# A selective-scan layer rearranged: channel halves outside, states inside, decays in PSUM, rows of B by DMA

## The reference

```python
x_dbl = jnp.einsum('bld,ed->ble', x, x_proj_w)        # x: layer-normed stream
delta_r = x_dbl[..., :DT_RANK]
B = x_dbl[..., DT_RANK:DT_RANK + D_STATE]
C = x_dbl[..., DT_RANK + D_STATE:]
delta = jax.nn.softplus(jnp.einsum('blr,dr->bld', delta_r, dt_proj_w) + dt_proj_b)
A = -jnp.exp(A_log)
dA = jnp.exp(delta[..., None] * A[None, None])
dBu = (delta * u)[..., None] * B[:, :, None, :]
def step(h, inp):
    dA_t, dBu_t, C_t = inp
    h = dA_t * h + dBu_t
    y_t = jnp.einsum('bdn,bn->bd', h, C_t)
    return (h, y_t)
return y + u * D[None, None, :]
```

## Time and profile before

| | us |
|---|---|
| median of 3 runs | 1988.52 (1988.13 to 1989.62) |
| the profiled execution, its own time | 1987.44 |
| its span in the trace | 1985.3 |
| the scan layer, first operation to last | 567.3 to 768.9 |
| its loop, first scan to last product | 610.4 to 759.35 |

### The profile page before, as it was taken

The page is one execution under the profiler, slowest core; times in us unless marked ns, Lnnn a source line. Parts: engine busy times, 40 slices in busy tenths (PEclk is TensorE's granted clock), DMA queues, the critical chain, the costliest instruction groups (busy, mean ns, idle before and its releaser), DMA issues. The chain is left out here.

```text
span 1985.3 us, 27571 instructions
## 1 busy us (share of the span) xinstructions
PE 1594.6 (80%) x9254; PEld 1163.6 (59%) x9254; DVE 1139.6 (57%) x2139; ACT 924.4 (47%) x1940; POOL 758.8 (38%) x699
## 2 busy tenths in 40 slices
PE   6999789778964656274899999999999999999373
PEld 5444578667841224263677677767777667776362
DVE  4665454755468996445655655556554665554533
ACT  2456334323524332243556555555665556665342
POOL 3011251215067674315633444344433443430603
PEclk9899789879977887596999999999999999999587
DMA  3222233223310003342000000000000000000443
GB/s 81 47 47 84 80 119 110 59 72 123 109 39 0 0 0 99 121 127 78 11 15 12 11 9 9 17 12 6 11 12 12 9 9 12 9 6 1 154 139 106
DMA packets 79204, 98.10 MB, mean 49 GB/s; under 512 B 12112, under 2 KB 63824, under 8 KB 79072
## 3 DMA queue, kind: packets, MB, share of 16 engines
q1 hardware_dynamic: 72928, 79.59, 13.8%
q0 software_dynamic: 6144, 16.79, 2.7%
HBM read 62.25 MB, written 27.66 MB: 45 GB/s over the span
## 5 line engine op out<-in xcount | busy, mean ns | idle before, releaser
L1307 DVE TENSOR_SCALAR_CACHE_REDUCE gqa_scaled<-acc,gqa_neg_scale 128x128 bf16<-128x128 f32 (+7 forms) x256 | 208.9, 816 | 312.4 <-PE acc L1459 311.0
L1479 PE MATMUL aux<-gqa_probsT,gqa_v 128*128 128x512 f32 (+3 forms) x768 | 272.1, 491 | 11.2 <-DVE gqa_turned_k L1263 7.0
L1200 ACT ACTIVATE gqa_probsT<-aux 128x512 f32<-128x512 f32 (+3 forms) x384 | 174.6, 491 | 188.0 <-PE aux L1470 188.0
L1190 ACT ACTIVATE gqa_probs<-acc,gqa_bias,gqa_q_scale 128x128 f32<-128x128 f32 (+7 forms) x256 | 213.7, 835 | 46.3 <-DVE gqa_scaled L1307 39.9
L1084 POOL TENSOR_TENSOR gqa_q_high<-gqa_straight,gqa_turned_q 128x512 fp32r<-128x512 f32 x64 | 87.7, 1370 | 327.7 <-DVE gqa_turned_q L1263 327.7
L1479 PEld LDWEIGHTS aux<-gqa_probsT,gqa_v 128*128 128x128 f32 x768 | 138.1, 190 | 103.1 <-issue 62.2
L1470 PE MATMUL aux<-ident,gqa_probs 128*128 128x128 f32 x1152 | 168.9, 274 | 0.3 <-ACT gqa_probsT L1200 0.3
L1458 PE MATMUL acc<-gqa_k_high,gqa_q_high 128*128 128x512 f32 (+3 forms) x384 | 156.4, 407 | 7.3 <-DVE gqa_k_low L1291 5.7
L1458 PE MATMUL acc<-gqa_k_high,gqa_q_low 128*128 128x512 f32 (+3 forms) x384 | 133.3, 347 | 0.0
L1458 PE MATMUL acc<-gqa_k_low,gqa_q_high 128*128 128x512 f32 (+3 forms) x384 | 132.9, 346 | 0.0
L1470 PEld LDWEIGHTS aux<-ident,gqa_probs 128*128 128x128 f32 x1152 | 124.7, 141 | 0.6 <-issue 0.4
(11 more groups left out here) (411 smaller groups left out, 4329.5 us busy)
## 6 DMA issues: line engine op xcount, KB each, us to landing
f_w<-in_f_up SPq DMA_DIRECT2D x64, 256.0 KB, 2.7
f_xs<-tokens_by_slot SPq DMA_DIRECT2D x108, 128.0 KB, 2.2
outputs_by_slot<-f_y_tile SPq DMA_DIRECT2D x108, 128.0 KB, 1.7
f_w<-in_f_down SPq DMA_DIRECT2D x64, 128.0 KB, 3.0
mat_qk<-mat_high SPq DMA_DIRECT2D x64, 64.0 KB, 2.3
gqa_w_q<-in_g_wq SPq DMA_DIRECT2D x32, 128.0 KB, 2.0
gqa_wo<-in_g_wo SPq DMA_DIRECT2D x32, 128.0 KB, 2.0
tokens_by_slot<-zeros SPq DMA_DIRECT2D x1, 3968.0 KB, 13.2
```

The costliest lines, as they stand in the source:

```text
L1190: act.activation(probs_of(t, 0, t + 1), scores(t), ACT.Exp, bias=bias[:, n % 16:n % 16 + 1], scale=q_scale[:, h // 2 % 2, h % 2 * NT + t:h ...
L1200: act.activation(turned_tile(t, a, b), aux[:, chunk(n, c) % 2, 0:(b - a) * P].rearrange("p (s w) -> p s w", w=P), ACT.Copy).then_inc(chunk ...
L1307: dve.tensor_scalar(scaled[:, 0:width(t)], scores(t), neg_scale[:, h // 2 % 2, h % 2 * NT + t:h % 2 * NT + t + 1], None, ALU.mult, ALU.min ...
L1479: last = pe.matmul(weigh_bank(half)[:, first:], v[:, h // GQ % 2, s, :], moving, start=s == 0, stop=s == 4 * half + 3)
```

## The change

The layer now goes over the halves outside and the 16 states inside: 32 steps m, of half m // 16 and state m % 16. Per step there is one decay, one product dbu, one scan, one product hc, one pair of spreads of C and one pair of sums.

- The decay tiles lie in PSUM (acc 2, 3 and aux 0, 1 in turn), written there by ACT's Exp. The sums take only acc 0 and 1, since one half is summed at a time; the first half's output is formed by DVE inside the loop, at step 17. `dbu` and `h` have three tiles, `hc` two.
- B is no longer spread by PE and copied by ACT. DVE copies the 16 rows of B to `b_rows`, SP writes them to a DRAM tensor and reads them back with each row repeated on all 128 partitions, in five groups of 1, 1, 2, 4 and 8 rows. `b_all` holds all 16 rows, and the second half uses them again.
- The projections use the pair `xnT_high`, `xnT_low` and weights split in the same way (`w_high` by ACT, `w_low` by POOL), three fp32r matmuls for each fp32 one before. B and C are projected in two halves, after and between the time steps.
- `pick` is 32 columns wide; the matmul repeats its column by a zero step.
- The product du of the first half moves from POOL to DVE, that of the second half to a place between POOL's steps 12 and 13. ACT's Abs and Exp are done half by half.
- The loop is written out; `pipeline` is not used.

The core of the diff:

```diff
-            pool.wait_ge(norm.rstd_ready, NT // 2)
-            pool.memset(pick[:, :, :], 0.0).then_inc(made, 1)
+            pool.memset(w_in_all[:, :, P + ROWS:2 * P], 0.0).then_inc(padded, 1)
+            pool.memset(pick[:, :], 0.0).then_inc(made, 1)
+            norm.gpsimd(pool)
+            pool.wait_ge(w_high_ready, 1)
+            pool.tensor_tensor(w_low[:, :, :], w_in_all[:, :, :], w_high[:, :, :].bitcast(F32), ALU.subtract).then_inc(w_low_ready, 1)
...
+            sp.wait_ge(rows_ready, 1)
+            sp.dma_start(rows_dram, b_rows[:, :]).then_inc(rows_out, 16)
+            sp.wait_ge(rows_out, 16)
+            for g, (first, last) in enumerate(GROUPS):
+                sp.dma_start(b_all[:, first:last, :],
+                             rows_dram[first:last, :].unsqueeze(0).to_broadcast([P, last - first, T])).then_inc(b_in[g], 16)
...
-            def multiply(i, j):
-                n = 4 * i + j
-                pool.wait_ge(b_ready, n + 1)
-                if not (start(i) and j < 2):
-                    pool.wait_ge(h_ready, 2 * n - 2)
-                for k in range(DC):
-                    pool.tensor_tensor(dbu[:, 2 * (j % 2) + k], du[:, k], b_all[:, j % 4], ALU.mult).then_inc(dbu_ready, 1)
+            def multiply(m):
+                k, n = state(m)
+                if n == 0:
+                    pool.wait_ge(du_ready, k + 1)
+                for g, (first, _) in enumerate(GROUPS):
+                    if k == 0 and n == first:
+                        pool.wait_ge(b_in[g], 16)
+                if m >= 3:
+                    pool.wait_ge(h_ready, m - 2)
+                pool.tensor_tensor(dbu[:, m % 3], du[:, k], b_all[:, n], ALU.mult).then_inc(dbu_ready, 1)
...
-                for k in range(DC):
-                    act.activation(decay[:, 2 * (j % 2) + k], delta[:, k], ACT.Exp,
-                                   scale=a[:, k, bass.ds(n, 1)]).then_inc(decay_ready, 1)
+                if m == 0:
+                    act.wait_ge(relu_ready, 1)
+                elif m == 1:
+                    act.wait_ge(split, 2)
+                else:
+                    act.wait_ge(h_ready, m - 1)
+                act.activation(two(decay_banks[m % 2]), delta[:, k], ACT.Exp, scale=a[:, k, n:n + 1]).then_inc(decay_ready, 1)
...
+            def scan(m):
+                if m >= 3:
+                    dve.wait_ge(hc_ready, m - 2)
+                dve.wait_ge(decay_ready, m + 1)
+                dve.wait_ge(dbu_ready, m + 1)
+                dve.tensor_tensor_scan(h[:, m % 3], two(decay_banks[m % 2]), dbu[:, m % 3], 0.0, ALU.mult, ALU.add).then_inc(h_ready, 1)
+
+            def times_c(m):
+                dve.wait_ge(c_spread, m + 1)
+                dve.wait_ge(h_ready, m + 1)
+                if m >= 2:
+                    dve.wait_ge(summed, m - 1)
+                dve.tensor_tensor(hc[:, m % 2], h[:, m % 3], two(c_banks), ALU.mult).then_inc(hc_ready, 1)
...
+            for m in range(STEPS_ALL + 1):
+                if m < STEPS_ALL:
+                    scan(m)
+                if m >= 1:
+                    times_c(m - 1)
+                if m == STATE + 1:
+                    finish(0)
+            finish(1)
...
+            for m in range(STEPS_ALL):
+                pe.wait_ge(hc_ready, m + 1)
+                if m + 1 < STEPS_ALL:
+                    spread_c(m + 1)
+                if m == STATE:
+                    pe.wait_ge(y_ready, 1)
+                sums(m)
```

More of the change, by code:

```diff
@@ L2311, in scan_layer @@
         bc_done = sem("bc_done")
+        rows_ready = sem("rows_ready")
+        rows_out = sem("rows_out")
+        b_in = [sem(f"b_in{g}") for g in range(len(GROUPS))]
         split = sem("split")
@@ L2408, in _ @@
+            for m in range(STEPS_ALL):
+                make_decay(m)
         @block.vector
@@ L2451, in _ @@
-            pipeline(dve, STATE, [(0, scan)], 4, lead=8)
-            dve.wait_ge(summed, STATE * DC)
-            for k in range(DC):
-                dve.scalar_tensor_tensor(z[:, k], core.xnT[:, k], channel[:, k, 1:2],
-                                         acc[:, 2 * k:2 * k + 2, :].rearrange("p a b -> p (a b)"),
-                                         ALU.mult, ALU.add).then_inc(y_ready, 1)
+            bc = two(bc_banks)[0:ROWS]
+            relu(0)
+            dve.wait_ge(bc_done, 2)
@@ L2486, in spread @@
-            def spread(bank, row, done):
-                for hf in range(2):
-                    last = pe.matmul(aux[:, bank + hf, :], pick[:, bass.ds(row, 1), :].rearrange("p a m -> p (a m)"),
-                                     parts[:, hf * HALF:(hf + 1) * HALF], start=True, stop=True)
-                last.then_inc(done, 1)
-            def spread_b(i, j):
-                if not (start(i) and j < 1):
-                    pe.wait_ge(b_ready, 4 * i + j)
-                spread(0, 4 * i + j, b_spread)
@@ L2497, in spread_c @@
-            def spread_c(i, j):
-                if not (start(i) and j < 1):
-                    pe.wait_ge(hc_ready, 2 * (4 * i + j))
-                spread(2, STATE + 4 * i + j, c_spread)
-            def sums(i, j):
-                for k in range(DC):
-                    pe.wait_ge(hc_ready, 2 * (4 * i + j) + k + 1)
-                    for hf in range(2):
-                        last = pe.matmul(acc[:, 2 * k + hf, :], core.ident[:, :], hc[:, 2 * (j % 2) + k, hf * HALF:(hf + 1) * HALF],
-                                         start=False, stop=False, skip_group_check=True)
-                    last.then_inc(summed, 1)
@@ L2510, in _, with project @@
-            pipeline(pe, STATE, [(0, spread_b), (1, spread_c), (2, sums)], 4, lead=8)
-            for q in range(NT // 2):
-                pe.wait_ge(y_ready, DC)
-                for t in (2 * q, 2 * q + 1):
-                    for k in range(DC):
+            pe.wait_ge(norm.low_ready, NT // 2)
+            pe.wait_ge(w_low_ready, 1)
+            def project(banks, first, rows, hf):
+                for k in range(DC):
+                    cols = slice(first, first + P)
+                    for m, (left, right) in enumerate(three(w_high[:, k, cols], w_low[:, k, cols],
+                                                            core.xnT_high[:, k, hf * HALF:(hf + 1) * HALF],
+                                                            core.xnT_low[:, k, hf * HALF:(hf + 1) * HALF])):
+                        last = pe.matmul(banks[0:rows, hf, :], left, right, start=k + m == 0, stop=(k, m) == (DC - 1, 2))
+                return last
@@ new lines, in time_step @@
+            def time_step(k):
+                for hf in range(2):
+                    last = pe.matmul(dt_banks[k][:, hf, :], w_dt[:, k, :], low[:, hf * HALF:(hf + 1) * HALF], start=True, stop=True)
+                last.then_inc(dt_done, 1)
+            project(low_banks, 0, P, 0)
+            project(low_banks, 0, P, 1).then_inc(low_done, 1)
+            project(bc_banks, P, P, 0).then_inc(bc_done, 1)
+            pe.wait_ge(low_ready, 1)
+            pe.wait_ge(w_dt_in, 16)
+            pe.wait_ge(norm.xnT_ready, NT // 2)
@@ new lines, in _, with spread_c, sums @@
+            time_step(0)
+            project(bc_banks, P, P, 1).then_inc(bc_done, 1)
+            time_step(1)
+            def spread_c(m):
+                row = STATE + state(m)[1]
+                for hf in range(2):
+                    last = pe.matmul(c_banks[:, hf, :], pick[:, row:row + 1].to_broadcast([P, P]),
+                                     parts[:, hf * HALF:(hf + 1) * HALF], start=True, stop=True)
+                last.then_inc(c_spread, 1)
+            def sums(m):
+                k, n = state(m)
+                for hf in range(2):
+                    last = pe.matmul(y_banks[:, hf, :], core.ident[:, :], hc[:, m % 2, hf * HALF:(hf + 1) * HALF],
+                                     start=n == 0, stop=n == STATE - 1)
+                last.then_inc(summed, 1)
```

179 lines of the change are left out of this document (91 added, 88 removed).

## The result

The changed kernel takes 1945.14 us (median of 4 runs, 1941.08 to 1950.12); the kernel before, on the same chip, 1989.07 (4 runs, 1988.13 to 1994.0). The ratio is 0.9776, 95% interval 0.9761 to 0.979: faster. The forecast was 1942 (1933 to 1958). The profiled execution took 1947.12, its span is 1945.3.

What follows compares the result with a forecast made beforehand. DVE was taken to bound the state loop, its scans taking turns with POOL. Gains of 41.2 (loop), 2.2 (ahead) and 2.8 (behind) took 1987.4 to 1941.2, plus 1.1 to the median: 1942 us, range 1933 to 1958.

Steps and rivals of the forecast that it cites:

- Loop: State loop of the scan layer: 32 steps of 3.33 us plus an output, 107.8 for 149.0, gain 41.2 us.
- the free scan: In the loop: with decay in PSUM the scan no longer takes turns with POOL's product; step of 3.33 us.
- the two bounds: Per loop step: scan and POOL product one after the other, 4.35 us, or the scan undisturbed by POOL.
- rival 2: In the loop: scan still takes turns with POOL, step 4.35, loop 32 us longer, 1974 us; chance 0.05.
- PSUM as a source: Loop scans: 62 cycles more fixed cost by the skill page, 0.065 us each, 2.1 in 32; left out of the sum.
- Ahead of the loop: Layer's start to first scan: earlier normalisation and projection, first scan at 608.2 instead of 610.4, gain 2.2 us.
- The chain of 13 operations: DVE's work just before the first scan: begins at 588.4, takes 13.7 us, until 602.1 if POOL does not interfere.
- The late end of the range: First scan between 602.1 and 608.4; 608.2 taken because DVE's operations would take turns with up to three POOL products.
- Behind the loop: After the last product: one half's sums and output instead of two, 6.7 us against 9.5, gain 2.8.
- B from DRAM: Five reads, 8192 KB: last lands 25 to 32 us after first issue, hidden with 0 to 13 us to spare.
- rival 1: Slow broadcast of B from DRAM: loop stalls once it takes over 38 us, 2045 us at the far bound; chance 0.10.
- Rival 3: In the loop: PE stays at 1.2 GHz, 4.37 us per step, 33 us more, 1975 us; chance 0.05.

Runs made afterwards that it cites:

- e1: The changed kernel with only the decay put back from PSUM to SBUF; 1979.81 us, ratio 0.9948 to the kernel before.
- e9: The kernel before, unedited, run and profiled again; 1989.27 us (1 run).
- e5: The kernel before with only the small `pick` table of 32 columns, its column repeated by a zero step; 1986.79 us, ratio 0.9983.
- e2: The changed kernel with POOL's second product also waiting for the end of DVE's chain ahead of the loop; 1942.47 us.

## Why the prediction was right

- **Loop**: 41.2 forecast, 40.9 measured (149.0 to 108.1). The step is 3.31, forecast 3.33, and the free scan was the right choice between the two bounds; e1 is the other bound, 142.3, where rival 2 said 32 us more and 34 came.
- **PSUM as a source**: the Trainium skill, page "VectorE: DVE Perf Modes", section "The TRN2 errata", gives a PSUM source 62 cycles more than an SBUF source, as an estimate 0.065 us more per scan. The trace does not bear it out: the scans take 2.26 to 2.30 from PSUM and at least 2.26 from SBUF, so at most 0.03 more at the median.
- **Ahead of the loop**: first scan forecast at 608.2 on the old clock, measured 610.78 - 2.7 = 608.1; gain 2.3 for 2.2. The chain of 13 operations began at 591.06 - 2.7 = 588.4, as forecast, and the three meetings with POOL cost 2.03 each, forecast 2.1. The late end of the range was right, for the reason given.
- **Behind the loop**: 2.8 forecast, 2.8 measured (12.4 to 9.6). The terms that the prediction names there add up to 5.85 us and not to its 6.7; waits between the engines, which it does not name, make up the rest (6.5 measured).
- **B from DRAM**: forecast to land 25 to 32 us after the first read's issue, at 618 to 625 on the old clock. The first read was issued at 595.41 and the last one landed near 618.3: 23 us, at 615.6 on the old clock, a little ahead of the range. No step waited for it, and rival 1 falls. The 8192 KB came at 365 GB/s. The Trainium skill, page "DMA: Bandwidth & Descriptors", section "Latency and other measured facts", reports 103 GB/s for rows that lie 4 or 8 MiB apart from partition to partition, and infers, without having verified it, that the streams then hit the same memory channel in step. The rows here are 4 KB each and are read by all partitions, and no run here shows such a pitch; one row read by all partitions is no slow case in this kernel.
- **PE's clock**: 1.2 GHz in the first pair of the loop (3.50 for four sums at 617.31), then full rate, at no cost that DVE shows. Rival 3 falls.
- **What was wrong**: the prediction said that it would be wrong if the later layers, which are not edited, moved by more than 2 us. In the profiled execution the layers behind the scan layer moved by 3.3 us and those ahead of it by 2.6: 5.9 in all (1779.6 in sum, 1773.7 before), which is why it stands at 1947.1 and not at 1941.2. The sum over the same layers is 1775.8 in e9 and 1777.1 in e5, without the change, and 1774.7 to 1779.7 in the kernels with it. The step that failed is the last one, from the edited layer to the whole time, which took the other layers as the profiled execution of before has them and added 1.1 us. That execution, with its masked attention at 1.00, was at the low end of what these layers take. And 2.0 of the 5.9 us are the first transfer behind the grouped attention, which lands late in every kernel that reads the rows of B alone. The median came 3 us above the forecast.

## What to carry to other kernels

Where one operation's durations come in two groups, look for what ran beside it; if two engines' rows overlap and each is longer by nearly the other's length, they take turns, and moving one operand of one of them to PSUM may be worth more than any reordering. An engine that gets ahead early can cost as much as one that is late: a wait that holds POOL back made the layer 3.2 us shorter (e2). Measure an edited stage against its own start, since unedited stages alone moved by some 6 us between executions here.

## What was not expected of the hardware

- Casts of one SBUF operand take turns with POOL as two-operand operations do: 0.68 alone, 2.71 beside a product.
- A gap of 4.93 us before one PE instruction cost twice: the gap, and sums of 3.78 in place of 1.88 behind it.
- The start of PE's full rate in the masked attention differs between executions of one kernel and moves that layer by 2.7 us, a tenth of a percent of the whole.
- The first transfer behind the grouped attention, far from the edited layer, lands after 1.6 to 1.8 us in five of the thirteen profiles and after 3.1 to 3.7 in the other eight, and which of the two goes with the kernel. Why is open.
